# The second norm of the first phase on GpSimd, in groups of 128x384

## The chip, the cores and the metric

One Trainium2 chip, one of its cores. The metric is the device time in microseconds of one execution of the whole kernel. GpSimd is called POOL in the rows, VectorE DVE, ScalarE ACT, TensorE PE (its weight loads PEld), SyncE SP.

## The reference, cut to what matters

The kernel computes two layers on an image batch of 8 x 96 x 128 x 128. The change lies in layer 0, between its convolution and its feed-forward network:

```python
x = x + _L0_conv_ref(_ln_c(x), ...)          # clusters: cosines, sigmoid, argmax mask, gather
t = _to_tokens(x)
t = t + _L0_ffn_ref(_ln_t(t), W1, b1, W2, b2)
x = _from_tokens(t, x)

def _ln_t(v, eps=1e-5):
    m = jnp.mean(v, axis=-1, keepdims=True)
    s = jnp.var(v, axis=-1, keepdims=True)
    return (v - m) / jnp.sqrt(s + eps)
```

The network quantizes its input to fp8 (5 exponent and 2 mantissa bits), multiplies, rounds, applies relu, quantizes again and multiplies again.

## The kernel before, in words

It has three phases, one after the other. The first (`phase_a`) does layer 0 and the first norm of layer 1, the second the depthwise convolutions, the third the rest of layer 1. Only the first is touched.

**Tiles.** The batch is cut into 32 quads (8 images x 4 quarters) of 4096 tokens with 96 channels. A quad in token order is a buffer `xT` of 128 partitions by 32 tokens x 96 channels (3072 fp32). It is handled in 8 groups of 4 tokens per partition (128x384, `CW` = 384, `TPC` = 4, `NK` = 8), and for some work in 2 halves of 16 tokens (128x1536).

**Steps and slots.** A step i works at five quads at once, software-pipelined: the feed-forward network of quad i, the output of the clustering and the statistics of the second norm for quad q1 = i + 1, cosines and similarity for q2 = i + 2, the cluster centres for q3 = i + 3, the load and the statistics of the first norm for q4 = i + 4, and the tail of layer 1's norm for p = i - 1. A step has nine slots, 0 to 8; the network's hidden layer takes group s in slot s, its output group s - 1. Each engine has its order written out by hand: `body` in the block of each engine, with tables such as `COS_AT` (cosines of half 0 in slot 3, of half 1 in slot 5), `SIM_AT` (similarity in slots 4 and 6), `OUT_AT`, `FWD_AT`, `NORM2_AT` (the second norm in slots 7 and 8) and `NORM3_LATE` (ScalarE's third norm of quad p in slots 2 and 3). Nothing plans the order at run time: an engine that waits holds up everything behind it in its list.

**The second norm.** VectorE takes the statistics of a group pair by pair (`pair_stats`, L178) into `ff.st`. GpSimd turns a half of them into `ff.rstd` (`ln2` calls `ln_stats`: a scaling, L163, and a power of -0.5, L166). Then VectorE's `dve_norm` centres a half of the quad into `xc` (L216) and scales it into `q8` as fp8 (L220), half 0 at the end of slot 7 and half 1 at the end of slot 8. TensorE's `pe_q8` (L258) turns the groups of `q8`; that of group 0 of the next quad stands at the end of the step, that of group s + 1 at the start of slot s. It waits for the half that holds the group (event `norm2`, 2 per quad).

**GpSimd's order in a step**, all of it in one list: `ln1(q3, 1)` and `r_by_side(q3, 1)`; `ln3(p, 1)` (L1135 to L1143); `inverse_norms(q2, 0)` and `(q2, 1)` (L1188 to L1205, three Newton steps for rn, which VectorE's `cosines` reads at L987); `ln3(i, 0)`; `scaled_sim(q2, 0)` (L1164); `ln2(q1, 0)`; `centres(q3)`; `scaled_sim(q2, 1)`, which waits for VectorE's similarity in slot 6 (L1014); `ln2(q1, 1)`; `ln1(q4, 0)` and `r_by_side(q4, 0)`. ScalarE's third norm (L856) waits for `ln3`.

Of the kernel before, what the change touches and what calls it, by code (L numbers as in the profile page):

```python
# [5 lines left out]
F32 = mybir.dt.float32  # L6
# [5 lines left out]
ALU = mybir.AluOpType  # L12
# [3 lines left out]
P = 128  # L16
B, C, H, W = 8, 96, 128, 128
# [5 lines left out]
NT = TOK // P  # L23
NK = 8
TPC = NT // NK
CH = TOK // NK
CW = TPC * C
# [74 lines left out]
def begun(unit):  # L102

    return unit.real
# [77 lines left out]
def per_token(t, n):  # L182

    return t.unsqueeze(2).to_broadcast([P, n, C])


class FeedForward:


    def __init__(self, nc, ctx, phase, ev, ring, xT, wts, idb):  # L190
        self.nc, self.ev, self.ring, self.xT, self.w, self.idb = nc, ev, ring, xT, wts, idb
        sb = lambda n, s, d: ctx.enter_context(nc.sbuf_tensor(phase + n, s, d))
        self.hid = ctx.enter_context(nc.psum_tensor(phase + "hid", [P, NJ * CH], F32))
        self.xc = sb("xc", [P, NT // 2, C], F32)
        self.q8 = sb("q8", [P, NT, C], FP8)
        self.q8c = sb("q8c", [C, 2, CH], BF16)
        self.h16 = sb("h16", [P, 2, NJ * CH], F16)
        self.hq = sb("hq", [P, 2, NJ * CH], F16)
        self.y16 = sb("y16", [P, 2, CW], F16)
        self.y16b = sb("y16b", [P, 2, CW], F16)  # L200
        self.st = sb("st2", [P, NT, 3], F32)
        self.rstd = sb("rstd2", [P, NT], F32)
# [2 lines left out]
        return self.xT[i.buf(len(self.xT))]  # L205


    def dve_norm(self, dve, i, half):
        ev, n, o = self.ev, NT // 2, half * (NT // 2)
        x = self.x_of(i)[:, o * C:(o + n) * C].rearrange("p (t c) -> p t c", c=C)  # L210

        dve.wait_ge(ev["ln2"], ev.at("ln2", i, half))
        if half:

            dve.wait_ge(ev["norm2"], ev.at("norm2", i, 0))
        dve.tensor_tensor(self.xc[:], x, per_token(self.st[:, o:o + n, 1], n),  # L216
                          ALU.subtract).then_inc(ev["cen2"], 1)
        dve.wait_ge(ev["cen2"], ev.at("cen2", i, half))
        dve.sem_inc(ev.passed, 1)
        dve.tensor_tensor(self.q8[:, o:o + n, :], self.xc[:], per_token(self.rstd[:, o:o + n], n),  # L220
                          ALU.mult, saturate=False).then_inc(ev["norm2"], 1)

    def dve_hidden(self, dve, i, k):
        ev, b = self.ev, k % 2
# [22 lines left out]
    def pe_q8(self, pe, step, i, k):  # L247
        ev, ring = self.ev, self.ring

        pe.wait_ge(ev["norm2"], ev.at("norm2", i, k // (NK // 2)))  # L250
        name, unit, pos = ring.before(step, "q8", k)
        if begun(unit):

            pe.wait_ge(ev[name], ev.at(name, unit, pos))
        pe.sem_inc(ev.passed, 1)
        bank = ring.bank("q8", k)
        for t in range(TPC):
            m = pe.matmul(bank[0:C, t * P:(t + 1) * P], self.q8[:, k * TPC + t, :], self.idb[:, :],  # L258
                          start=True, stop=True)
        m.then_inc(ev["q8_full"], 1)  # L260
# [60 lines left out]
class SplitFeedForward(FeedForward):  # L321


    def __init__(self, nc, ctx, phase, ev, ring, xT, wts, idb):
        self.nc, self.ev, self.ring, self.xT, self.w, self.idb = nc, ev, ring, xT, wts, idb
        sb = lambda n, s, d: ctx.enter_context(nc.sbuf_tensor(phase + n, s, d))
        self.hid2 = [ctx.enter_context(nc.psum_tensor(phase + f"hid{p}", [P, CH], F32)) for p in range(2)]
        self.xc = sb("xc", [P, NT // 2, C], F32)
        self.q8 = sb("q8", [P, NT, C], FP8)
        self.q8c = sb("q8c", [C, 2, CH], BF16)  # L330
        self.h16 = sb("h16", [P, 2, NJ * CH], F16)
        self.hq = sb("hq", [P, 2, NJ * CH], F16)
        self.y16 = sb("y16", [P, 2, CW], F16)
        self.y16b = sb("y16b", [P, 2, CW], F16)
        self.st = sb("st2", [P, NT, 3], F32)
        self.rstd = sb("rstd2", [P, NT], F32)
# [26 lines left out]
    def dve_hidden(self, dve, i, k):  # L363
        ev, b = self.ev, k % 2
        for j in range(NJ):
# [7 lines left out]
        dve.tensor_scalar(u, u, ROUND8, ROUND8, ALU.add, ALU.subtract).then_inc(ev["hq"], 1)  # L373


FFN_EVENTS = dict(x1=NK, bn2=NK, ln2=2, ln2_s=2, cen2=2, norm2=2, q8_full=NK, y_full=NK, c_full=NK, q8c=NK, hidden=NK, h16=NK,
                  relu=NK, hq=NK, y16=NK, yb=NK, x2=NK, cout=NK)


# [37 lines left out]
COS_AT = {3: 0, 5: 1}  # L417
SIM_AT = {4: 0, 6: 1}
SIMT_AT = {5: 0, 7: 1}
NORM2_AT = {7: 0, 8: 1}  # L420
SIDE_AT, STD_AT, MEAN_AT, CF_AT, CN2_AT, CW_AT = 2, 2, 3, 4, 5, 8
AGG_AT, SUM_AT, VAL_AT, PA_AT = 8, 0, 1, 2
NORM3_AT, NORM3_LATE = {7: (0, 1), 8: (2, 3)}, {2: (4, 5), 3: (6, 7)}
# [2 lines left out]
def phase_a(nc, consts, x, wf_t, wf, bf, wv_t, bv, wp_t, bp, alpha, beta, w1, b1, w2, b2, gamma, beta_ln, x2_dram, x3_dram):  # L426
# [4 lines left out]
    with ExitStack() as ctx:  # L431
        sb = lambda n, s, d: ctx.enter_context(nc.sbuf_tensor(n, s, d))
# [108 lines left out]
        ff = SplitFeedForward(nc, ctx, "A_", ev, back, xT, wts, idb)  # L541
# [387 lines left out]
        def _(dve):  # L929
# [122 lines left out]
            def body(i):  # L1052
                q1, q2, q3, q4, p = i + 1, i + 2, i + 3, i + 4, i - 1
                for s in range(FFN_SLOTS):
# [40 lines left out]
                    if q3.real and s == CW_AT:  # L1095

                        dve.wait_ge(ev["cw"], ev.at("cw", q3, 0))
                        dve.tensor_copy(big_w[:, C:BIGN], s_cw).then_inc(ev["cwc"], 1)  # L1098
                    if q1.real and s in NORM2_AT:
                        ff.dve_norm(dve, q1, NORM2_AT[s])  # L1100

            steps(dve, body)

# [1 line left out]
        def _(pool):  # L1105
# [9 lines left out]
            def ln2(q, half):  # L1115

                pool.wait_ge(ev["bn2"], ev.at("bn2", q, 4 * half + 3))
                pool.sem_inc(ev.passed, 1)
                ln_stats(pool, ev, "ln2", ff.st, ff.rstd, var[1], expo, q, half, EPS_T, 1.0)

# [24 lines left out]
            def r_by_side(q, h):  # L1145

                pool.wait_ge(ev["ln1"], ev.at("ln1", q, h))
                pool.sem_inc(ev.passed, 1)
                if begun(q - 1):

                    pool.wait_ge(ev["side"], ev.at("side", q - 1, 0))
                    pool.sem_inc(ev.passed, 1)
                n = NT // 2
                w = slice(h * n, (h + 1) * n)
                pool.tensor_tensor(rmask[:, w, 2 * h:2 * h + 2], rstd1[q.buf(NB)][:, w].unsqueeze(2).to_broadcast([P, n, 2]),
                                   side.unsqueeze(1).to_broadcast([P, n, 2]), ALU.mult).then_inc(ev["rmask"], 1)
# [50 lines left out]
            def body(i):  # L1207
                q1, q2, q3, q4, p = i + 1, i + 2, i + 3, i + 4, i - 1
                if q3.real:
                    ln1(q3, 1)  # L1210
                    r_by_side(q3, 1)
                if p.real:
                    ln3(p, 1)
                for h in range(2):
                    if q2.real:
                        inverse_norms(q2, h)

                        pool.wait_ge(ev["rn"], ev.at("rn", q2, h))
                        pool.sem_inc(ev.passed, 1)
                if i.real:  # L1220
                    ln3(i, 0)
                if q2.real:
                    scaled_sim(q2, 0)
                if q1.real:
                    ln2(q1, 0)
                if q3.real:
                    centres(q3)
                if q2.real:
                    scaled_sim(q2, 1)
                if q1.real:  # L1230
                    ln2(q1, 1)
                if q4.real:
                    ln1(q4, 0)
                    r_by_side(q4, 0)

            steps(pool, body)


# [636 lines left out]
```

## Time and profile before

| what | us |
|---|---|
| median of 3 runs (range) | 4150.91 (4149.14 to 4152.14) |
| the profiled execution | 4150.77 |
| its span, first to last instruction | 4149.2 |
| first phase, about | 0 to 2105 |

| engine, whole span | busy us | share |
|---|---|---|
| PE | 3270.8 | 79% |
| PEld | 2521.2 | 61% |
| DVE | 3025.8 | 73% |
| ACT | 2745.2 | 66% |
| POOL | 1425.2 | 34% |

The slices of the profile, 40 of 103.7 us each, show the phases; a digit is the busy share in tenths, the first phase is the first twenty:

```
DVE  4888888888888888888852222222288988988987
ACT  2577777777777777777762222222189999999998
POOL 3555655556555565555420000000022222222221
PEclk8788888888888888888769999999889999999999
```

A share is an average over work with different limits. In the first phase no engine is busy all the time, so the order inside one step has to be read.

### The profile page before, as it was taken

Reading aid. Unit: us, or ns where it says so; the run is one execution under the profiler, and the core shown is the slowest. Engines: PE = TensorE matmul, PEld = TensorE weight load, DVE = VectorE, ACT = ScalarE, POOL = GpSimd, SP = SyncE. Lnnn points to the kernel's source line nnn. Section 1 sums busy time; section 2 is a strip of 40 time slices with the busy share of each in tenths; the row PEclk is TensorE's granted clock in tenths of the full one; section 3 lists DMA queues with packets and bytes.
Section 4 is the critical chain, followed back from the end, with each engine's and each line's share of the span. In section 5 each row is a group of like instructions: output and inputs, shape, how many; then the busy total and the mean of one; then the engine's idle time right before and its main releaser. Section 6 shows DMA issues by size and latency. Waiting matters only on the chain. (4 is left out here: it accounts for less than half of the span.)

```text
span 4149.2 us, 80812 instructions
## 1 busy us (share of the span) xinstructions
PE 3270.8 (79%) x26660; PEld 2521.2 (61%) x26660; DVE 3025.8 (73%) x7852; ACT 2745.2 (66%) x6274; POOL 1425.2 (34%) x1892
## 2 busy tenths in 40 slices
PE   6767677776777767777659999999788778787777
PEld 5655555555555555555539999999744444444443
DVE  4888888888888888888852222222288988988987
ACT  2577777777777777777762222222189999999998
POOL 3555655556555565555420000000022222222221
PEclk8788888888888888888769999999889999999999
DMA  3133232332323323232235566566576666666662
GB/s 64 45 77 81 73 77 62 77 80 74 78 62 77 80 75 77 62 78 64 60 102 160 159 165 167 159 165 167 155 199 183 178 177 184 180 180 182 180 180 79
DMA packets 733898, 490.45 MB, mean 118 GB/s; under 512 B 420797, under 2 KB 712957, under 8 KB 721277
## 3 DMA queue, kind: packets, MB, share of 16 engines
q1 hardware_dynamic: 733564, 486.32, 44.5%
q8 instruction: 171, 2.80, 0.3%
q14 instruction: 163, 1.33, 0.1%
HBM read 284.42 MB, written 201.33 MB: 117 GB/s over the span
## 5 line engine op out<-in xcount | busy, mean ns | idle before, releaser
L1794 POOL TENSOR_SCALAR C_var<-C_st 128x16 f32<-128x16 f32 x64 | 16.3, 254 | 1697.4 <-DVE C_st L178 1697.4
L1331 PE MATMUL B_ps_row<-B_g,B_z 128*128 128x128 f32 x4608 | 555.8, 277 | 0.6 <-ACT B_g L1363 0.6
L1331 PEld LDWEIGHTS B_ps_row<-B_g,B_z 128*128 128x128 f32 x4608 | 532.1, 193 | 0.7 <-ACT B_g L1363 0.7
L361 ACT ACTIVATE A_h<-A_hid 128x512 f16<-128x512 f32 x768 | 426.5, 591 | 66.7 <-PE A_hid L348 63.1
L1424 DVE TENSOR_TENSOR B_mid<-B_ps_row,B_row_bias 128x512 f32<-128x512 f32 x192 | 132.8, 691 | 458.3 <-PE B_ps_row L1331 448.3
L166 POOL TENSOR_TENSOR A_rstd<-A_var,A_expo 128x16 f32<-128x16 f32 x128 | 454.2, 3549 | 23.7 <-POOL A_var L163 23.6
L178 DVE BATCH_NORM_STATS2 A_st<-A_xT 128x6 f32<-128x192 f32 x1536 | 443.6, 349 | 24.8 <-ACT A_xT L826 11.5
L361 ACT ACTIVATE C_h<-C_hid 128x512 f16<-128x512 f32 x768 | 426.1, 592 | 15.0 <-PE C_hid L348 7.7
L1461 ACT ACTIVATE C_q<-C_xT,C_shift,C_rstd 128x96 fp8e5<-128x96 f32 x1024 | 391.4, 456 | 40.9 <-POOL C_shift L1801 40.9
L369 DVE TENSOR_SCALAR A_hq<-A_h,A_b 128x512 f16<-128x512 f16 x768 | 250.0, 363 | 198.3 <-ACT A_h L361 193.3
L856 ACT ACTIVATE A_xc<-A_xT,A_shift,A_rstd 128x96 f32<-128x96 f32 x1024 | 379.0, 456 | 0.0
L663 PEld LDWEIGHTS A_fbank<-A_big_w,A_xq 97*128 97x128 f32 x2048 | 337.0, 236 | 63.4 <-DVE A_big_w L1098 29.5
L663 PE MATMUL A_fbank<-A_big_w,A_xq 97*128 97x112 f32 x2048 | 333.9, 318 | 23.2 <-DVE A_big_w L1098 21.7
L1375 ACT ACTIVATE B_y<-B_ps_col,B_col_bias 128x512 f32<-128x512 f32 x192 | 132.0, 687 | 318.1 <-PE B_ps_col L1342 318.1
L348 PE MATMUL A_hid<-A_q8c,A_w 96*128 96x512 bf16 x768 | 313.4, 467 | 31.6 <-ACT A_h L361 29.5
L288 PE MATMUL A_bbank<-A_w,A_hq 128*128 128x96 f16 x3072 | 218.9, 234 | 121.7 <-DVE A_hq L373 73.6
L1645 PE MATMUL C_fbank<-C_y3q,C_pw 96*96 96x512 f32 x512 | 279.5, 629 | 43.1 <-DMA C_y3q<-y_scratch 23.4
L288 PEld LDWEIGHTS A_bbank<-A_w,A_hq 128*128 128x128 f16 x3072 | 189.2, 114 | 188.4 <-DVE A_hq L373 119.3
L348 PE MATMUL C_hid<-C_q8c,C_w 96*128 96x512 bf16 x768 | 262.7, 390 | 49.9 <-ACT C_h L361 43.3
L369 DVE TENSOR_SCALAR C_hq<-C_h,C_b 128x512 f16<-128x512 f16 x768 | 243.1, 346 | 74.1 <-ACT C_h L361 67.8
L296 ACT ACTIVATE A_q8c<-A_bbank 96x512 bf16<-96x512 f32 x256 | 149.8, 586 | 192.6 <-PE A_bbank L258 191.0
L746 PE MATMUL A_fbank<-A_pabd,A_simT 128*128 128x384 f32 x512 | 234.6, 587 | 35.5 <-DVE A_xT L1050 35.5
(162 smaller groups left out, 7509.5 us busy)
## 6 DMA issues: line engine op xcount, KB each, us to landing
A_xq<-in_x SPq DMA_DIRECT2D x32, 1536.0 KB, 8.9
x_scratch<-A_xT SPq DMA_DIRECT2D x64, 768.0 KB, 3.2
x_scratch<-A_x3h SPq DMA_DIRECT2D x64, 768.0 KB, 5.4
B_z<-x_scratch SPq DMA_DIRECT2D x96, 512.0 KB, 5.0
y_scratch<-B_y SPq DMA_DIRECT2D x96, 512.0 KB, 3.7
C_x3q<-x_scratch SPq DMA_DIRECT2D x32, 1536.0 KB, 9.2
C_y3q<-y_scratch SPq DMA_DIRECT2D x32, 1536.0 KB, 15.7
C_xT<-x_scratch SPq DMA_DIRECT2D x64, 768.0 KB, 15.9
```

Source lines behind the costliest of these rows:

```text
L166: m = pool.tensor_tensor(rstd[:, o:o + n], var[:], expo[:, 0:n], ALU.pow)
L178: return dve.bn_stats(st[:, n:n + 2, :].rearrange("p t s -> p (t s)"), x[:, n * C:(n + 2) * C].rearrange("p (t c) -> p c t", t=2))
L288: m = pe.matmul(bank[:, t * C:(t + 1) * C], self.hq[:, b, s:s + P], self.w["w2"][:, j, :], start=(j == 0), stop=(j == NJ - 1))
L348: pe.matmul(self.hid2[n % 2][:], self.w["w1"][:, j * P:(j + 1) * P], self.q8c[:, k % 2, :], start=True, stop=True).then_inc(ev["hidden"], 1)
L361: act.activation(self.h16[:, k % 2, j * CH:(j + 1) * CH], self.hid2[n % 2][:], ACT.Copy).then_inc(ev["h16"], 1)
L369: r = dve.tensor_scalar(self.hq[:, b, s], self.h16[:, b, s], self.w["b1"][:, j:j + 1], 0.0, ALU.add, ALU.max)
L663: m = pe.matmul(bank[:, t * BIGN:(t + 1) * BIGN], xq[q.buf(NX)][:, n * P:(n + 1) * P], big_w[:, :], start=True, stop=True)
L746: pe.matmul(front.bank("out", k)[:, 0:CW], simT[q.buf(2)][:, k, :], pabd[:], start=True, stop=True).then_inc(ev["out_full"], 1)
L856: m = act.activation(xc3[:, k // 4, t % (NT // 2), :], xT[u.buf(NB)][:, t * C:(t + 1) * C], ACT.Identity, scale=rstd3[:, t:t + 1], bias=sh ...
L1331: m = pe.matmul(ps_row[h][:, b * P:(b + 1) * P], z[c.buf(NB)][:, h * HB + b, d:d + W], g[c.buf(2)][:, d, :], start=(d == 0), stop=(d == 2))
L1461: m = act.activation(self.q8[:, t, :], x[:, t * C:(t + 1) * C], ACT.Identity, scale=self.rstd[:, t:t + 1], bias=self.shift[:, t:t + 1], sa ...
L1645: pe.matmul(rows(front.bank("pw", k)[0:C, 0:CH]), pw[:], group(y3q[q.buf(2)], k), start=True, stop=True).then_inc(ev["pw_full"], 1)
```

## The change

`dve_norm` and its table `NORM2_AT` are gone. `pool_norm` does the same arithmetic on GpSimd, a half per call and within it a group at a time: centring (subtract the mean) of group k + 1 is put ahead of scaling (multiply by rstd, to fp8) of group k, with two group buffers in `xc`. The call for half 0 of quad q1 stands in GpSimd's list behind `ln2(q1, 1)`, the call for half 1 of quad i near the start of the list, behind `r_by_side(q3, 1)` and ahead of `ln3(p, 1)`. The events `cen2` and `norm2` count 8 per quad in place of 2, and TensorE waits for the group it reads. `ln2` waits until the norm of the quad before has read `rstd`.

```diff
-        self.xc = sb("xc", [P, NT // 2, C], F32)
+        self.xc = sb("xc", [P, 2, TPC, C], F32)
...
-    def dve_norm(self, dve, i, half):
-        ev, n, o = self.ev, NT // 2, half * (NT // 2)
-        x = self.x_of(i)[:, o * C:(o + n) * C].rearrange("p (t c) -> p t c", c=C)
-
-        dve.wait_ge(ev["ln2"], ev.at("ln2", i, half))
-        if half:
-
-            dve.wait_ge(ev["norm2"], ev.at("norm2", i, 0))
-        dve.tensor_tensor(self.xc[:], x, per_token(self.st[:, o:o + n, 1], n),
-                          ALU.subtract).then_inc(ev["cen2"], 1)
-        dve.wait_ge(ev["cen2"], ev.at("cen2", i, half))
-        dve.sem_inc(ev.passed, 1)
-        dve.tensor_tensor(self.q8[:, o:o + n, :], self.xc[:], per_token(self.rstd[:, o:o + n], n),
-                          ALU.mult, saturate=False).then_inc(ev["norm2"], 1)
+    def pool_norm(self, pool, i, half):
+        ev, x = self.ev, self.x_of(i)
+        first = half * NK // 2
+
+        def centred(k):
+            if k >= 2:
+
+                pool.wait_ge(ev["norm2"], ev.at("norm2", i, k - 2))
+            elif begun(i - 1):
+                pool.wait_ge(ev["norm2"], ev.at("norm2", i - 1, NK - 2 + k))
+            t = slice(k * TPC, (k + 1) * TPC)
+            pool.tensor_tensor(self.xc[:, k % 2], x[:, k * CW:(k + 1) * CW].rearrange("p (t c) -> p t c", c=C),
+                               per_token(self.st[:, t, 1], TPC), ALU.subtract).then_inc(ev["cen2"], 1)
+
+        def scaled(k):
+
+            pool.wait_ge(ev["cen2"], ev.at("cen2", i, k))
+            if begun(i - 1):
+
+                pool.wait_ge(ev["q8_full"], ev.at("q8_full", i - 1, k))
+            t = slice(k * TPC, (k + 1) * TPC)
+            pool.tensor_tensor(self.q8[:, t, :], self.xc[:, k % 2], per_token(self.rstd[:, t], TPC), ALU.mult,
+                               saturate=False).then_inc(ev["norm2"], 1)
+
+        pool.wait_ge(ev["ln2"], ev.at("ln2", i, half))
+        centred(first)
+        for k in range(first, first + NK // 2):
+            if k + 1 < first + NK // 2:
+                centred(k + 1)
+            scaled(k)
...
-        pe.wait_ge(ev["norm2"], ev.at("norm2", i, k // (NK // 2)))
+        pe.wait_ge(ev["norm2"], ev.at("norm2", i, k))
...
-                    if q1.real and s in NORM2_AT:
-                        ff.dve_norm(dve, q1, NORM2_AT[s])
...
                 pool.wait_ge(ev["bn2"], ev.at("bn2", q, 4 * half + 3))
+                if begun(q - 1):
+
+                    pool.wait_ge(ev["norm2"], ev.at("norm2", q - 1, 4 * half + 3))
...
                     ln1(q3, 1)
                     r_by_side(q3, 1)
+                if i.real:
+                    ff.pool_norm(pool, i, 1)
                 if p.real:
                     ln3(p, 1)
...
                     ln2(q1, 1)
+                    ff.pool_norm(pool, q1, 0)
                 if q4.real:
                     ln1(q4, 0)
```

## Rows read from the trace of the kernel before

**Rows 1.** One line's instructions, 300 to 2000 us: count, min/median/max ns, first and last start.

```profile
L1014 DVE TENSOR_TENSOR A_sim<-A_sim,A_eq x53: 424/425/426, 302.7 to 1987.8; 128x256 f32<-128x256 f32 x53
```

**Rows 2.** Stretches of one step: length, busy us (instructions) by engine, granted clock, DMA share, GB/s.

```profile
1016.53:1031.93 15.40, 11.99 (x141) 10.11 (x141) 14.94 (x32) 11.68 (x27) 11.98 (x9) 0.82 0.24 75
1031.93:1049.69 17.76, 14.43 (x155) 12.85 (x155) 12.57 (x36) 11.49 (x31) 11.46 (x20) 0.71 0.12 26
1049.69:1081.38 31.69, 20.93 (x155) 14.19 (x155) 28.21 (x86) 23.70 (x55) 13.78 (x23) 0.87 0.44 101
```

**Rows 3.** VectorE in order of time: start, us, instruction, count, [idle before <-releaser].

```profile
1016.11 0.42 DVE L1014 TENSOR_TENSOR A_sim<-A_sim,A_eq 128x256 f32<-128x256 f32 x1
...
1021.38 1.75 DVE L216 TENSOR_TENSOR A_xc<-A_xT,A_st 128x1536 f32<-128x1536 f32 x1
1023.28 1.76 DVE L220 TENSOR_TENSOR A_q<-A_xc,A_rstd 128x1536 fp8e5<-128x1536 f32 x1 [0.15 <-DVE A_xc L216]
...
1028.36 1.75 DVE L216 TENSOR_TENSOR A_xc<-A_xT,A_st 128x1536 f32<-128x1536 f32 x1
1030.26 1.76 DVE L220 TENSOR_TENSOR A_q<-A_xc,A_rstd 128x1536 fp8e5<-128x1536 f32 x1
...
1049.69 0.23 DVE L987 TENSOR_TENSOR A_rn<-A_rn,A_guard 128x64 f32<-128x64 f32 x1
...
1059.82 0.35 DVE L369 TENSOR_SCALAR A_hq<-A_h,A_b 128x512 f16<-128x512 f16 x1 [2.16 <-ACT A_h L361]
```

**Rows 4.** GpSimd in order of time, same step; then the spread of L163.

```profile
1016.71 0.62 POOL L1164 TENSOR_TENSOR A_simr<-A_sim,A_rstd 128x256 f32<-128x256 f32 x1 [6.30 <-DVE A_sim L1014]
...
1017.73 2.90 POOL L166 TENSOR_TENSOR A_rstd<-A_var,A_expo 128x16 f32<-128x16 f32 x1 [0.18 <-POOL A_var L163]
1021.23 0.21 POOL L163 TENSOR_SCALAR A_var<-A_st 128x16 f32<-128x16 f32 x1 [0.60 <-DVE A_st L178]
1021.63 4.26 POOL L166 TENSOR_TENSOR A_rstd<-A_var,A_expo 128x16 f32<-128x16 f32 x1 [0.18 <-POOL A_var L163]
...
1028.43 1.75 POOL L163 TENSOR_SCALAR A_var<-A_st 128x16 f32<-128x16 f32 x1 [1.63 <-DVE A_st L178]
1030.37 4.41 POOL L166 TENSOR_TENSOR A_rstd<-A_var,A_expo 128x16 f32<-128x16 f32 x1 [0.18 <-POOL A_var L163]
...
1039.54 0.64 POOL L1143 TENSOR_TENSOR A_shift<-A_less,A_rstd 128x16 f32<-128x16 f32 x1 [0.18 <-POOL A_rstd L1140]
1041.97 0.26 POOL L1188 TENSOR_SCALAR A_guard<-A_rstd 128x16 f32<-128x16 f32 x1 [1.79 <-DVE A_seed L978]
...
1047.88 0.32 POOL L1205 TENSOR_TENSOR A_rn<-A_newton 128x64 f32<-128x64 f32 x1 [0.18 <-POOL A_newton L1202]
...
L163 POOL TENSOR_SCALAR A_var<-A_st x109: 207/263/1779, 303.9 to 2094.5; 128x16 f32<-128x16 f32 x109
```

**Rows 5.** ScalarE in order of time, same step: third norm in slot 2, slot 3's first copy.

```profile
1045.44 2.96 ACT L856 ACTIVATE A_xc<-A_xT,A_shift,A_rstd 128x96 f32<-128x96 f32 x8
...
1048.60 0.57 ACT L296 ACTIVATE A_q8c<-A_bbank 96x512 bf16<-96x512 f32 x1
```

**Rows 6.** GpSimd's nearest passes: one line's instructions, columns as in rows 1.

```profile
L1164 POOL TENSOR_TENSOR A_simr<-A_sim,A_rstd x55: 618/622/787, 303.3 to 2046.7; 128x256 f32<-128x256 f32 x55
...
L1205 POOL TENSOR_TENSOR A_rn<-A_newton x52: 317/320/323, 334.5 to 1967.5; 128x64 f32<-128x64 f32 x52
```

**Rows 7.** VectorE's spread, 300 to 2100 us: one line's instructions, columns as in rows 1.

```profile
L991 DVE TENSOR_TENSOR A_dots<-A_dots,A_rn x54: 424/576/890, 336.6 to 2033.3; 128x256 f32<-128x256 f32 x54
...
L369 DVE TENSOR_SCALAR A_hq<-A_h,A_b x675: 330/346/772, 303.0 to 2094.6; 128x512 f16<-128x512 f16 x169
...
L373 DVE TENSOR_SCALAR A_hq<-A_hq x225: 559/560/857, 304.4 to 2095.0; 128x1536 uint16<-128x1536 uint16 x113
...
L240 DVE TENSOR_TENSOR A_y16b<-A_y,A_b x225: 343/351/455, 304.9 to 2095.5; 128x384 f16<-128x384 f16 x113
...
L244 DVE TENSOR_TENSOR A_xT<-A_xT,A_y16b x225: 557/558/667, 305.3 to 2095.9; 128x384 f32<-128x384 f32 x113
```

More of the change, by code:

```diff
@@ L327, in __init__ @@
         self.hid2 = [ctx.enter_context(nc.psum_tensor(phase + f"hid{p}", [P, CH], F32)) for p in range(2)]
-        self.xc = sb("xc", [P, NT // 2, C], F32)
+        self.xc = sb("xc", [P, 2, TPC, C], F32)
         self.q8 = sb("q8", [P, NT, C], FP8)
@@ L373, in dve_hidden @@
         dve.tensor_scalar(u, u, ROUND8, ROUND8, ALU.add, ALU.subtract).then_inc(ev["hq"], 1)
-FFN_EVENTS = dict(x1=NK, bn2=NK, ln2=2, ln2_s=2, cen2=2, norm2=2, q8_full=NK, y_full=NK, c_full=NK, q8c=NK, hidden=NK, h16=NK,
+FFN_EVENTS = dict(x1=NK, bn2=NK, ln2=2, ln2_s=2, cen2=NK, norm2=NK, q8_full=NK, y_full=NK, c_full=NK, q8c=NK, hidden=NK, h16=NK,
                   relu=NK, hq=NK, y16=NK, yb=NK, x2=NK, cout=NK)
@@ L419 @@
 SIMT_AT = {5: 0, 7: 1}
-NORM2_AT = {7: 0, 8: 1}
 SIDE_AT, STD_AT, MEAN_AT, CF_AT, CN2_AT, CW_AT = 2, 2, 3, 4, 5, 8
```

## The prediction

> **What bounds the kernel now.** I read the slices and the stretches first, then one steady step on each engine in order of time, then the spread of single instructions. The first phase ends at about 2105 us and is a loop over 32 quads; the change touches nothing behind it. Its period is 64.8 us: the last pass of the similarity of a quad half (L1014) comes 53 times between 302.7 and 1987.8 us, two to a step, so 1685.1 / 26 [rows 1]. I call S the end of its second half in slot 6 (1016.53 in the step read) and divide the step there. From S to the first cosines of the next step (L987, slot 3, 1049.69) are 33.2 us, from there to the next S 31.7 us [rows 2, 3]. In the second part VectorE is busy for 28.2 of 31.7 us and its only long wait, 2.16 us, is for ScalarE: VectorE bounds it. In the first part it is busy almost throughout up to the end of slot 8 (14.9 of 15.4 us), then 12.6 of 17.8 us while it follows ScalarE and TensorE [rows 2, 3].
>
> GpSimd is busy for 12.0 + 11.5 + 13.8 = 37.3 of 64.8 us [rows 2]. Its share says there is room for the new passes. What decides is where they stand in its order, since it is served in order by a written list, and two others wait for its results: VectorE's cosines of slot 3 need the inverse norms (L1205 to A_rn), and ScalarE's third norm in slot 2 needs the rstd and shift of ln3 (L1143). Today these come in time: the inverse norms end at 1048.20 with the cosines at 1049.69, and ln3's shift ends at 1040.18 with its reader at 1045.44 [rows 3, 4, 5].
>
> **What is removed.** Four passes of 128x1536 on VectorE per step: 2 x 1.75 + 2 x 1.76 = 7.0 us, all of them between S and slot 3 [rows 3]. They lie on the path today: behind them VectorE copies the summed rows and starts the next slot. So VectorE would be at slot 3 up to 7.0 us earlier; with the order of ScalarE and TensorE as it stands I expect half of that to come back as waits for ScalarE: it arrives between S + 26.2 (33.2 - 7.0, no new wait) and S + 33.2 (all of it given back), say S + 29.5.
>
> **What is added.** Sixteen passes of 128x384 on GpSimd per step, eight at the end of the list (half 0 of the next quad, behind ln2) and eight near its start (half 1, behind ln1 and ahead of ln3 and of both inverse norms). No such pass is in the trace. The nearest rows are the pass of 128x256 with a broadcast operand, 0.618 at the least, 0.622 in the median, and the one of 128x64, 0.320 [rows 6]. Their slope is 0.302 / 192 = 1.57 ns an element, which gives 0.62 + 128 x 0.00157 = 0.82 us for 384. The lower bound is 0.62 (it can't be shorter than the smaller pass); the upper is 0.622 x 384 / 256 = 0.93 with nothing fixed in it. The scaling pass writes fp8 instead of fp32, and no row shows that on GpSimd; VectorE's own passes differ by 0.02 us for it [rows 3], so I add nothing and keep 1.0 us as an outer end. The GPSIMD Engine Reference of the Trainium skill (section Performance versus the Vector engine) gives 4497 ns for 2048 elements, an estimate of 0.84 us for 384 by proportion; by it the sum below would be 0.3 us longer a step. Waiting for the instruction just ahead costs GpSimd 0.18 us each time; a half has two or three such places. So a half costs 8 x 0.82 + 3 x 0.18 = 7.1 us, or 6.9, together 14.0 us.
>
> **The chain on GpSimd from S to the cosines.** Today: scaled similarity, ln2, ln1 of half 0, ln1 of half 1, ln3, inverse norms, from 1016.53 to 1048.20, 31.7 us [rows 3, 4]. Three idle times in it vanish when the engine runs late: 0.60 before L163, 1.63 between 1026.80 and 1028.43, and 1.79 before L1188, 4.0 us. Three of its instructions are long today because VectorE's big passes run: L163 takes 1.75 in place of 0.25 and ends with the L216 beside it (1030.18 against 1030.11), and L166 takes 4.26 and 4.41 where it takes 2.90 alone, both beside an L216 or L220 [rows 3, 4]. With those passes gone this gives back 1.50 + 1.36 + 1.51 = 4.4 us. So 31.7 - 4.0 - 4.4 + 14.0 = 37.3 us, and with 0.1 to VectorE 37.4 us. VectorE can be there at S + 29.5. It therefore stands at slot 3 for about 8 us in every step, and ScalarE stands in slot 2: ln3 ends ahead of the inverse norms by their 6.2 us (1041.97 to 1048.20), at S + 31.2, where ScalarE gets to its reader at S + 28.9 today (1045.44) and would some 3 us earlier now. From ln3's end ScalarE needs 2.96 and 0.2 us to slot 3's first copy [rows 5], so at S + 34.4 it is 3.0 us ahead of the cosines, against 1.1 us today: this lead takes most of the 2.16 us wait in slot 4 [rows 3, 5]. The second part becomes 30.0 us (between 29.5 and 31.7).
>
> **Waits for the port.** The row of L163 shows what a GpSimd read meets when VectorE runs with two SBUF inputs: it ends when VectorE's does. The other way round, L991 takes 0.424 at the least but 0.576 in the median and 0.890 at most, and L369 up to 0.772 for 0.346 [rows 4, 7]. So the two engines wait for each other's whole instructions, and the new passes will meet those of VectorE. Of that kind VectorE has in each slot 3 x 0.35 + 0.56 + 0.35 + 0.56 = 2.5 us (L369, L373, L240, L244) [rows 7]. SBUF — State Buffer of the Trainium skill (section Who interferes with whom) says the same as a rule: a VectorE instruction with two SBUF inputs or in a two-port mode and a GpSimd one that reads SBUF exclude each other for a whole instruction. While half 0 is normed (S + 4 to S + 12) VectorE has an addition pair (L240, L244) and part of a hidden block in its way, 1.5 us; while half 1 is normed (about S + 22 to S + 30) more than one slot's worth, 2.7 us. I take 4.2 us a step for both, between 0 (every pass in a gap) and 8 us (each of the 16 passes held for most of an instruction of 0.56). What VectorE itself loses, half a pass of 0.82 each time, falls ahead of its stall in slot 3 and costs nothing.
>
> **The sum.** Period 37.4 + 4.2 + 30.0 = 71.6 us, 6.8 more than today. The chain has both ln1 calls and both norms in the steps i = 0 to 28, 29 of them: +197 us. The last three steps lack ln1 and the inverse norms, so VectorE's relief counts there, between 0 and 21 us; I take 10. The profiled execution is 4150.8 us with a span of 4149.2, and the median of the runs is 4150.9, so no correction between them: 4150.8 + 197 - 10 = 4338, about 4340 us.
>
> The other edits cost nothing I can find. TensorE's wait by group (k in place of the half) waits for group 0, done after ln2 (S + 4.1) and three passes, S + 7; today the half is done at 1025.04, S + 8.5 [rows 3]. Groups 4 to 7 are done when ln3 begins, S + 27 to S + 31, and are first asked for in slot 3. The new wait of ln2 on the norms of the last quad is over long before. Nothing of the DMA queues moves: the stores of x2 and x3 only follow the later steps.
>
> **The rivals.**
> 1. The chain binds, but the port waits are near nothing and the pass takes 0.82: period 37.4 + 30.0 = 67.4, so 29 x 2.6 - 10 = +65, 4216 us. For it: the last instruction of the inverse norms hardly varies beside a busy VectorE (317 to 323 ns) [rows 6]. Against: L163's row.
> 2. The passes are slow: 1.0 us each (+2.9 a step), 6 us of port waits and no gain of lead: 37.4 + 2.9 + 6 + 31.7 = 78.0, 29 x 13.2 - 10 = +373, 4524 us. It needs fp8 output to be dear on GpSimd or VectorE to win the port always.
> 3. The other side: the norm is hidden on GpSimd and VectorE's relief counts. It decides at the chain's length: with 30.0 us behind it, the period falls below 64.8 once the sixteen passes and their port waits take less than 11.4 us (0.66 us a pass, no port wait); at the bound of 0.62 it gives 64.2, 29 x -0.6 - 10 = -27, about 4123 us. Were it fully hidden, VectorE at S + 29.5 would give 61.1, 3.7 less in 29 steps, 4040 us. The slope of rows 6 speaks against both.
> 4. Nearly no change, 4150 within 8 us: the narrow strip between rivals 1 and 3.
>
> **Chances.** Forecast (4260 to 4450) 0.62; rival 1 (4160 to 4260) 0.15; rival 2 (above 4450) 0.12; rival 3 0.07; rival 4 0.04. The range 4190 to 4460 leaves out about 2 in 10. A measurement of this kernel can tell about 0.2% (8 us) from no change: faster 0.07, same 0.04, slower 0.89.
>
> **What the profile after would show.** L216 and L220 gone from VectorE; sixteen passes of 0.8 to 1.0 us on GpSimd per step, with a longer tail where VectorE works; L166 back at 2.9 us; VectorE before L987 idle for 7 to 12 us a step with GpSimd's A_rn as releaser (today: none); ScalarE before L856 waiting for A_shift L1143; GpSimd's idle before L1188 nearly gone; TensorE's granted clock lower in slot 3. I am wrong if L987 has no wait, if the pass takes under 0.66 us, or if the stall comes elsewhere, at q8 of a group.

## The result, and the profile after

The changed kernel takes 4266.59 us (median of 4 runs, 4264.12 to 4268.1) against 4150.89 before: 1.0278 times as long, 95% interval 1.0261 to 1.0296. It is slower by 116 us. The prediction said slower, 4340 us, range 4190 to 4460; the direction and the place were right, the size was too large by 73 us.

The whole loss lies in the first phase: the last similarity of a quad (L1014, now L1029) starts at 2160.9 us in place of 2046.1, and VectorE's first instruction of the second phase comes at 2281.3 in place of 2161.0.

The same two stretches of a step as in [rows 2], of the kernel after (S to the cosines, cosines to the next S; columns as there):

```profile
1004.23:1041.58 37.35, 27.64 (x303) 24.61 (x304) 24.37 (x62) 24.74 (x62) 32.57 (x44) 0.77 0.16 44
1041.58:1072.85 31.27, 21.74 (x150) 14.83 (x149) 28.15 (x87) 21.20 (x48) 13.71 (x23) 0.83 0.44 101
```

The first stretch was 33.2 us and is 37.35, the second was 31.7 and is 31.3. Over the 24 to 26 steady steps between 300 and 2100 us, with S (the end of the similarity) and the start of the first cosines taken for each step, the means are 33.2 + 31.7 before (period 64.8) and 37.6 + 30.9 after (period 68.55). All means by step below are worked out in this way. The stretch from S to the cosines is called the first part below, the rest of the step the second part.

Waits of the kernel after, 300 to 2100 us (engine, line waited for: us in total, times, longest):

```profile
DVE A_rn L1002 <- POOL A_rn L1221: 140.1, 26, 6.2
...
ACT A_xc L871 <- POOL A_shift L1159: 146.6, 26, 6.3
```

VectorE waits for the inverse norms in slot 3, 140.1 / 26 = 5.4 us a step, where the line before (L987) had no wait in these steps. ScalarE waits for ln3 in slot 2, 5.6 us a step. Each is one wait per step.

GpSimd's list in the same step, in order of time (start, us, instruction, count), and the spread of the two new passes, 300 to 2100 us (min/median/max ns):

```profile
1004.40 0.62 POOL L1180 TENSOR_TENSOR A_simr<-A_sim,A_rstd 128x256 f32<-128x256 f32 x1 [6.30 <-DVE A_sim L1029]
...
1008.29 1.83 POOL L219 TENSOR_TENSOR A_xc<-A_xT,A_st 128x384 f32<-128x384 f32 x2
...
1015.86 2.90 POOL L166 TENSOR_TENSOR A_rstd<-A_var,A_expo 128x16 f32<-128x16 f32 x1 [0.18 <-POOL A_var L163]
...
1041.23 0.32 POOL L1221 TENSOR_TENSOR A_rn<-A_newton 128x64 f32<-128x64 f32 x1 [0.18 <-POOL A_newton L1218]
...
L219 POOL TENSOR_TENSOR A_xc<-A_xT,A_st x208: 825/832/1227, 322.9 to 2057.0; 128x384 f32<-128x384 f32 x104
L229 POOL TENSOR_TENSOR A_q<-A_xc,A_rstd x208: 818/827/1142, 324.7 to 2059.0; 128x384 fp8e5<-128x384 f32 x104
```

A pass takes 0.83 us in the median, with fp8 output too. One pass in three takes longer, up to 1.23 us; the mean is 0.91 us. From S (1004.23) the chain runs to the end of the inverse norms at 1041.55 with no pause longer than 0.28 us. The power of ln1 is back at 2.90 us where [rows 4] had 4.26 and 4.41.

VectorE in the same step:

```profile
1024.33 1.07 DVE L389 TENSOR_SCALAR A_hq<-A_hq 128x1536 uint16<-128x1536 uint16 x1
...
1028.14 1.07 DVE L260 TENSOR_TENSOR A_xT<-A_xT,A_y16b 128x384 f32<-128x384 f32 x1
...
1029.85 2.10 DVE L385 TENSOR_SCALAR A_hq<-A_h,A_b 128x512 f16<-128x512 f16 x3
...
1041.58 0.23 DVE L1002 TENSOR_TENSOR A_rn<-A_rn,A_guard 128x64 f32<-128x64 f32 x1 [5.20 <-POOL A_rn L1221]
```

Beside the passes of half 1 (1024.0 to 1031.5) VectorE's instructions take twice their time and more: 1.07 for 0.56, 2.10 for 0.87. In the whole first part it is busy for 24.4 us, where the kernel before has 27.5 with 7.0 of them in the norm [rows 2, 3]: 3.9 us more for the same instructions. It pays for the port, and then stands 5.20 us in slot 3 anyhow.

### The profile page after: what moved, and what is told of

It is laid out like the page before. It is cut to its first block and busy times, and to the rows that moved or that the text cites. A ratio compares the mean times of both kernels' runs of the same rounds, so it can differ in the third digit from the quotient of the medians.

```text
span 4266.2 us, 81411 instructions
## 1 busy us (share of the span) xinstructions
PE 3273.9 (77%) x26660; PEld 2544.5 (60%) x26660; DVE 2921.9 (68%) x7724; ACT 2744.7 (64%) x6274; POOL 1728.3 (41%) x2404
## 5 line engine op out<-in xcount | busy, mean ns | idle before, releaser
L385 DVE TENSOR_SCALAR A_hq<-A_h,A_b 128x512 f16<-128x512 f16 x768 | 288.9, 413 | 281.6 <-ACT A_h L377 274.7
L364 PE MATMUL A_hid<-A_q8c,A_w 96*128 96x512 bf16 x768 | 291.2, 434 | 196.5 <-ACT A_h L377 194.6
L166 POOL TENSOR_TENSOR A_rstd<-A_var,A_expo 128x16 f32<-128x16 f32 x128 | 377.9, 2953 | 24.0 <-POOL A_var L163 24.0
L678 PEld LDWEIGHTS A_fbank<-A_big_w,A_xq 97*128 97x128 f32 x2048 | 354.1, 248 | 33.1 <-issue 8.4
L678 PE MATMUL A_fbank<-A_big_w,A_xq 97*128 97x112 f32 x2048 | 351.1, 331 | 4.9 <-DVE A_pabd L1058 3.5
L304 PEld LDWEIGHTS A_bbank<-A_w,A_hq 128*128 128x128 f16 x3072 | 198.5, 117 | 198.0 <-DVE A_hq L389 112.9
L761 PE MATMUL A_fbank<-A_pabd,A_simT 128*128 128x384 f32 x512 | 247.5, 615 | 29.9 <-DVE A_xT L1065 29.9
L1382 ACT ACTIVATE B_g<-B_ps_g 128x384 f32<-128x384 f32 x96 | 47.2, 491 | 303.4 <-PE B_ps_c L1337 303.4
```

The lines of the kernel that those rows point to most:

```text
L166: m = pool.tensor_tensor(rstd[:, o:o + n], var[:], expo[:, 0:n], ALU.pow)
L304: m = pe.matmul(bank[:, t * C:(t + 1) * C], self.hq[:, b, s:s + P], self.w["w2"][:, j, :], start=(j == 0), stop=(j == NJ - 1))
L364: pe.matmul(self.hid2[n % 2][:], self.w["w1"][:, j * P:(j + 1) * P], self.q8c[:, k % 2, :], start=True, stop=True).then_inc(ev["hidden"], 1)
L385: r = dve.tensor_scalar(self.hq[:, b, s], self.h16[:, b, s], self.w["b1"][:, j:j + 1], 0.0, ALU.add, ALU.max)
L678: m = pe.matmul(bank[:, t * BIGN:(t + 1) * BIGN], xq[q.buf(NX)][:, n * P:(n + 1) * P], big_w[:, :], start=True, stop=True)
L761: pe.matmul(front.bank("out", k)[:, 0:CW], simT[q.buf(2)][:, k, :], pabd[:], start=True, stop=True).then_inc(ev["out_full"], 1)
```

## The experiments

Two theories were to be told apart. **Order:** the loss is the place of the sixteen passes in GpSimd's list, inside the chain from S to the inverse norms; VectorE's relief is real but spent as waiting. **Amount of work and port:** GpSimd has got too much to do, or holds the port too long, wherever the passes stand. Each time stands beside 7 to 17 runs of the kernel before on the same chip (medians 4150.0 to 4151.6).

### VectorE's relief alone

```diff
+        x, n = x[:, 0:1, :], 1
-        dve.tensor_tensor(self.xc[:], x, per_token(self.st[:, o:o + n, 1], n),
+        dve.tensor_tensor(self.xc[:, 0:1, :], x, per_token(self.st[:, o:o + n, 1], n),
...
-        dve.tensor_tensor(self.q8[:, o:o + n, :], self.xc[:], per_token(self.rstd[:, o:o + n], n),
+        dve.tensor_tensor(self.q8[:, o:o + n, :], self.xc[:, 0:1, :], per_token(self.rstd[:, o:o + n], n),
```

> The kernel before, with VectorE's four passes of the second norm cut from 128x1536 to 128x96 (the rest of the norm is left out, the waits stay). No pass goes to GpSimd. It prices VectorE's relief alone. Order theory (what the changed kernel lost, it lost by the place of its passes in GpSimd's list; the relief itself is real): VectorE spends about 1 instead of 7 us on the norm, reaches slot 3 at S + 30 in place of S + 33.2, the second part stays at 31.3 us, so the period is 61 to 62 us against 64.8 and the whole 4050 to 4080 us. Rival (ScalarE and TensorE set the first part anyway, so that VectorE's relief is worth next to nothing and the changed kernel could only lose): 4130 to 4150 us.

Measured 4054.34 us, ratio 0.9769 (0.9753 to 0.9786), in the expected range. Stretches of one step:

```profile
1032.91:1063.28 30.37, 25.44 (x297) 22.29 (x297) 21.79 (x68) 22.81 (x58) 18.80 (x28) 0.80 0.19 54
1063.28:1094.22 30.94, 20.63 (x155) 14.15 (x154) 28.27 (x87) 22.85 (x53) 13.62 (x23) 0.89 0.45 103
```

The mean period is 61.4 us. Six microseconds less on VectorE shorten the first part by 2.8 us (33.2 to 30.4): less than half counts, the rest comes back as waits for ScalarE and TensorE. The relief is worth 97 us, so the changed kernel had something to win.

### The same passes elsewhere in GpSimd's list

Half 0 behind ln2 of half 0, where GpSimd waits:

```diff
                     ln2(q1, 0)
+                    ff.pool_norm(pool, q1, 0)
...
                     ln2(q1, 1)
-                    ff.pool_norm(pool, q1, 0)
```

> The changed kernel with the norm of half 0 of the next quad moved in GpSimd's list from behind ln2 of half 1 to behind ln2 of half 0, where the engine waits for VectorE for 2.3 and 6.3 us. The same sixteen passes, the same waits. Order theory: the chain from S to the inverse norms is shorter by 7.1 us, 30.2 us, so VectorE arrives last, at S + 31; the passes now meet VectorE where it is the bound and cost it 1 to 3 us there; period 63.5 to 65.5, the whole 4110 to 4175 us. Rival (the loss comes from the amount of work on GpSimd and the port it holds, wherever it stands): 4250 to 4280 us, as changed.

Groups 5 to 7 of half 1 behind the inverse norms (`pool_norm` takes its first group and a count):

```diff
                 if i.real:
-                    ff.pool_norm(pool, i, 1)
+                    ff.pool_norm(pool, i, 1, 4, 1)
...
                         pool.wait_ge(ev["rn"], ev.at("rn", q2, h))
                         pool.sem_inc(ev.passed, 1)
+                    if i.real:
+                        ff.pool_norm(pool, i, 1, 5 + h, 1 + h)
```

> The changed kernel with three of the four groups of half 1 taken out of the chain in GpSimd's list: group 4 stays, group 5 goes behind the first inverse norms, groups 6 and 7 behind the second. Order theory: the chain from S is shorter by three groups, 5.3 us, 32.0 us, as long as VectorE needs to get there (S + 32.2); the wait at the cosines, 5.4 us a step, goes; period 63.5 to 65, the whole 4115 to 4160 us. Rival (amount of work and port): 4250 to 4280 us.

Both moves:

> Both moves together: half 0 behind ln2 of half 0, groups 5 to 7 behind the inverse norms. Order theory: the chain from S is 24.9 us and no longer binds anywhere; VectorE does, with 6 us less work and what it loses by the port: period 61.5 to 64.5, the whole 4060 to 4140 us, below e2 and e3 only if VectorE's arrival is not what ends the first part in those. Rival (amount of work and port): 4250 to 4280 us.

Measured 4181.60 us with half 0 early (e2; ratio 1.0076, 1.0060 to 1.0093), 4154.22 us with groups 5 to 7 late (e3; 1.0007, 0.9997 to 1.0016) and 4206.74 us with both (e4; 1.0132, 1.0115 to 1.0149). One step of each, in this order:

```profile
1026.68:1058.74 32.06, 26.68 (x296) 23.59 (x296) 22.57 (x64) 22.87 (x58) 25.68 (x36) 0.76 0.18 51
1058.74:1093.35 34.61, 21.73 (x155) 15.10 (x155) 31.08 (x87) 23.76 (x56) 20.64 (x31) 0.80 0.40 92
```

```profile
1020.13:1052.52 32.39, 27.42 (x318) 24.28 (x319) 22.66 (x62) 24.72 (x64) 27.40 (x38) 0.81 0.18 51
1052.52:1084.99 32.47, 17.88 (x134) 11.96 (x132) 30.30 (x87) 21.98 (x49) 19.63 (x29) 0.87 0.43 99
```

```profile
1040.25:1071.55 31.30, 26.34 (x296) 23.33 (x296) 21.45 (x63) 22.84 (x58) 21.97 (x32) 0.77 0.19 52
1071.55:1107.93 36.38, 24.37 (x155) 16.79 (x155) 33.13 (x87) 24.09 (x56) 25.05 (x36) 0.73 0.39 88
```

With the same sixteen passes the loss falls from 116 us to 30, to 3 and to 55. The first part shrinks each time, in the mean from 37.6 to 31.3, 32.2 and 30.6 us, as the order theory says; the amount-of-work theory, which expected 4250 to 4280 in all three, falls. But the second part grows, from 30.9 to 34.0, 32.6 and 35.8 us, and VectorE's busy time in it, in the steps shown, from 28 to 31, 30 and 33 us for the same 87 instructions. There VectorE is the bound, and the passes are beside it. The port half of the rival is therefore right in that part: e2 and e4 lie above what I expected (4110 to 4175, 4060 to 4140), since I had priced the meeting at 1 to 3 us.

Two waits are left in e3 that its expectation did not have. VectorE still stands for the inverse norms, 52.1 / 26 = 2.0 us a step. And TensorE waits for the late groups of `q8` in the second part, 134.8 us in the 26 steps, 5.2 a step (e4: 61.7 us, 2.4). VectorE is busy there for 30.3 of 32.5 us, so this second wait can account for 2.2 us at most; no run takes it away by itself.

### The port by itself

The kernel before with eight passes that nobody uses, behind ln2 of half 0:

```diff
+            def extra(q):
+                for k in range(8):
+                    if k >= 2:
+                        pool.wait_ge(ev["dum"], ev.at("dum", q, k - 2))
+                    elif begun(q - 1):
+                        pool.wait_ge(ev["dum"], ev.at("dum", q - 1, 6 + k))
+                    pool.tensor_tensor(scr[:, k % 2], scr_in[:], per_token(expo[:, 0:TPC], TPC),
+                                       ALU.mult).then_inc(ev["dum"], 1)
...
                     ln2(q1, 0)
+                    extra(q1)
```

> The kernel before, whole, with eight more passes of 128x384 on GpSimd that nobody uses, with two SBUF operands, behind ln2 of half 0, where GpSimd waits for VectorE for more than their 7.1 us. They prolong no chain. Port theory (what e2, e3 and e4 lost behind the cosines is VectorE waiting for the port): VectorE's instructions there take 2.5 to 3.5 us a step longer, period 67.3 to 68.3, the whole 4225 to 4265 us. Rival (e2 and e4 lost it because results of GpSimd, the centres and the scaled similarity, came later or because of TensorE's lower clock): 4150 to 4180 us.

And the same with fills in place of the passes:

```diff
+                    pool.memset(scr[:, k % 2], 0.0).then_inc(ev["dum"], 1)
```

> As the run with eight unused passes, but the passes only write (a fill of 128x384), so they read nothing from SBUF. Port theory with a lock of the reading side for instructions with two SBUF operands and of both sides for the fast one-operand forms: the additions (L240, L244) keep their 0.35 and 0.56 us, the fast forms (L369, L373) still wait; the loss is half of that with reading passes or less, 4160 to 4210 us. If any GpSimd instruction shuts VectorE out: as with reading passes, in proportion to the fills' length. If no write does: 4145 to 4160 us.

Measured 4256.18 us with passes (1.0261, 1.0243 to 1.0278) and 4153.56 us with fills (1.0006, 0.9997 to 1.0016). With the passes, the second stretch of a step, VectorE in slot 6, and the pass's spread:

```profile
1032.83:1067.90 35.07, 22.11 (x155) 15.20 (x155) 31.53 (x87) 23.77 (x56) 20.55 (x31) 0.79 0.39 91
```

```profile
1056.09 2.53 DVE L369 TENSOR_SCALAR A_hq<-A_h,A_b 128x512 f16<-128x512 f16 x3
1058.65 1.06 DVE L373 TENSOR_SCALAR A_hq<-A_hq 128x1536 uint16<-128x1536 uint16 x1
1059.64 0.98 DVE L240 TENSOR_TENSOR A_y16b<-A_y,A_b 128x384 f16<-128x384 f16 x1
1060.65 1.06 DVE L244 TENSOR_TENSOR A_xT<-A_xT,A_y16b 128x384 f32<-128x384 f32 x1
...
L1216 POOL TENSOR_TENSOR A_scr<-A_scr_in,A_expo x200: 821/870/1138, 303.2 to 1947.8; 128x384 f32<-128x384 f32 x100
```

Four lines of VectorE take 2.53 + 1.06 + 0.98 + 1.06 = 5.6 us, where slot 5 of the same step has 0.87 + 0.56 + 0.35 + 0.56 = 2.3. These 3.3 us are nearly all of the 3.4 us by which the mean second part is longer (35.0 against 31.7); the mean period is 68.2 against 64.8. GpSimd's passes themselves stay at 0.87 us in the median, 0.90 in the mean, for 0.82 at the least. No data depended on these passes. The cluster centres behind them in the list end some 5 us later in the step (30.5 us behind the first cosines in place of 25.7), but between 300 and 2000 us no other engine waits for any result of GpSimd. So this is the price of the port alone: 106 us.

With fills, these are their spread and VectorE's, 300 to 2000 us:

```profile
L1216 POOL MEMSET A_scr<- x208: 412/413/608, 357.1 to 1981.2; 128x384 f32 x104
...
L369 DVE TENSOR_SCALAR A_hq<-A_h,A_b x627: 332/347/1385, 303.0 to 1989.0; 128x512 f16<-128x512 f16 x157
...
L240 DVE TENSOR_TENSOR A_y16b<-A_y,A_b x210: 337/351/500, 304.8 to 1995.0; 128x384 f16<-128x384 f16 x105
...
L244 DVE TENSOR_TENSOR A_xT<-A_xT,A_y16b x210: 557/558/666, 305.2 to 1995.3; 128x384 f32<-128x384 f32 x105
```

The additions with two SBUF inputs (L240, L244) reach 0.50 and 0.67 us at most, much as in [rows 7] (0.46 and 0.67), where the reading passes held them up to 0.98 and 1.07. The fast one-input form (L369) is held, up to 1.39 us for 0.35. So a write shuts out the fast form and a read both. SBUF — State Buffer of the Trainium skill (section Who interferes with whom) states this split; the trace agrees. The fills cost nothing in all, 3 us within the interval, less than I had expected of the fast forms (4160 to 4210 us). By the time alone the case in which no write shuts VectorE out (4145 to 4160) would have won; the row of L369 speaks against it. The second part does get longer, 32.3 us in the mean for 31.7, and the first gives the same back, 32.5 for 33.2; why it does was not tried.

### A microsecond in the chain

The changed kernel with the same fills, which cost nothing elsewhere, put ahead of ln3:

```diff
                 if i.real:
                     ff.pool_norm(pool, i, 1)
+                if i.real:
+                    extra(i)
                 if p.real:
                     ln3(p, 1)
```

> The changed kernel with the eight unused fills of 128x384 (0.413 us each, the ones that cost nothing behind ln2 of half 0) put ahead of ln3, inside the chain. They shut nobody out of SBUF. Order theory: every microsecond there is a microsecond of the period: 8 x 0.413 = 3.3 us a step, the whole 4345 to 4385 us. Port or amount-of-work rival: 4260 to 4275 us.

Measured 4365.43 us (1.0516, 1.0500 to 1.0533), 99 us more than the changed kernel. VectorE's wait for the inverse norms, 300 to 2000 us:

```profile
DVE A_rn L1005 <- POOL A_rn L1224: 164.3, 23, 9.0
```

7.1 us a step in place of 5.4, and a mean period of 71.7 against 68.55, 3.1 us for 3.3 us of fills. Free in one place of the list, paid nearly in full in another: this shows the chain as the cause, without the reading side of the port. The expectation says that the fills shut nobody out of SBUF; the row of L369 above shows that VectorE's fast form does wait for them, which cost nothing there in all.

### The wait by group

```diff
-        pe.wait_ge(ev["norm2"], ev.at("norm2", i, k))
+        pe.wait_ge(ev["norm2"], ev.at("norm2", i, 4 * (k // 4) + 3))
```

> The changed kernel with TensorE waiting again for the half that holds the group (the fourth norm of the half in place of its own). Order theory: q8 of group 0 then goes at S + 11.3 in place of S + 8.7, which shifts slots 0 to 2 by up to 2.6 us, but GpSimd's chain ends 5.4 us behind VectorE: same time, 4255 to 4280 us. Rival (the group wait is what kept the loss small): 2 us or more a step, above 4320 us.

Measured 4245.34 us (1.0229, 1.0213 to 1.0245): 21 us less than the changed kernel, which neither theory said. TensorE does wait for the half, 300 to 2000 us:

```profile
PE A_bbank L274 <- POOL A_q L229: 68.9, 25, 3.2
```

2.8 us a step, and yet the mean period is 67.4 us (66.0 to 68.7 from step to step) with 37.3 + 30.1. So the finer wait did not keep the loss small. Most of the gain stands in the second part, where VectorE waits 0.7 us a step for ScalarE's copies (A_h) in place of 1.6; and GpSimd's passes take 0.88 us in the mean in place of 0.91. Why the coarse wait does this is open; the later start changes where TensorE idles and with that its granted clock, but nothing here isolates that.

### One half only

Half 1 on VectorE in slot 8, half 0 on GpSimd as changed (the other half's call dropped, each engine with events of its own):

```diff
                     if q1.real and s == 8:
+                        ff.dve_norm(dve, q1, 1)
...
-                if i.real:
-                    ff.pool_norm(pool, i, 1)
```

> Half of the change: half 0 is normed on GpSimd as in the changed kernel (behind ln2 of half 1), half 1 stays with VectorE in slot 8, in passes of 128x1536. Order theory: GpSimd's chain from S is 23.4 + 7.1 = 30.5 us, but VectorE's two passes of slot 8 meet GpSimd's and hold them up to 3.5 us, 31 to 34; VectorE itself arrives at S + 31.5 to 32.5; behind it 31.0. Period 63 to 65, the whole 4090 to 4155 us. Amount-of-work rival: half way between before and changed, 4205 us.

Half 0 on VectorE in slot 7, half 1 on GpSimd as changed:

```diff
                     if q1.real and s == 7:
+                        ff.dve_norm(dve, q1, 0)
...
                     ln2(q1, 1)
-                    ff.pool_norm(pool, q1, 0)
```

> The other half of the change: half 1 is normed on GpSimd as in the changed kernel (ahead of ln3), half 0 stays with VectorE in slot 7, in passes of 128x1536. Order theory: the chain from S is 23.4 + 6.9 + 1.5 for the passes of slot 7 = 31.8 us, VectorE arrives at S + 31.5 to 32.5, behind it 31.0: period 62.7 to 63.8, the whole 4080 to 4120 us, a little below the kernel before and below e5. Amount-of-work rival: 4205 us.

Measured 4136.98 us for the first (e5; 0.9969, 0.9959 to 0.9980) and 4129.63 us for the second (e6; 0.9952, 0.9936 to 0.9969), 10 us above what I had expected of it. Both beat the kernel before by a little, 0.3 and 0.5%; half the work moved is not half the loss, the amount-of-work theory's 4205 is out. One step of the second:

```profile
1009.29:1042.61 33.32, 27.39 (x313) 23.91 (x314) 24.87 (x65) 24.72 (x62) 26.62 (x36) 0.81 0.18 49
1042.61:1072.59 29.98, 19.58 (x141) 12.89 (x139) 28.32 (x87) 21.70 (x51) 14.27 (x23) 0.90 0.47 107
```

In the mean 33.8 + 30.2: the chain still ends last (VectorE waits 84.5 / 26 = 3.3 us a step for it), 2.0 us later than I had summed, since GpSimd's idle times of 0.60 and 1.63 us had come back, and the gain lies in the second part. There VectorE's wait for ScalarE's copies (A_h) falls from 2.35 us a step before the change to 0.8.

### Half 1 before the second ln1

```diff
                     r_by_side(q3, 1)
-                if i.real:
-                    ff.pool_norm(pool, i, 1)
...
                     ln1(q4, 0)
                     r_by_side(q4, 0)
+                if q1.real:
+                    ff.pool_norm(pool, q1, 1)
```

> The kernel with half 0 on VectorE and half 1 on GpSimd (e6), with the norm of half 1 moved from behind the second ln1 to ahead of it, at the end of the step before, into the 1.63 us in which GpSimd waits for VectorE's statistics. Order theory: the chain from S shrinks from 33.7 to 32 us, VectorE arrives at 31.5 to 32: period 62.0 to 62.8 against 64.0, the whole 4070 to 4100 us. If VectorE already ended the first part in e6: 4120 to 4135 us. It is the version that may beat both kernels.

Measured 4150.16 us (1.0000, 0.9991 to 1.0009): a miss. GpSimd's chain did shrink to 32.3 us and VectorE no longer waits for it, but VectorE comes only at S + 32.8 itself (33.0 in the mean), and the second part is 31.8 us in place of 30.2: VectorE waits 2.5 us a step there for ScalarE's copies in place of 0.8. VectorE in slot 0, then the wait of TensorE that hangs on it, here and in the kernel of half 1 (e6), 300 to 2000 us:

```profile
1025.70 1.66 DVE L402 TENSOR_SCALAR A_hq<-A_h,A_b 128x512 f16<-128x512 f16 x2
...
1028.14 0.96 DVE L402 TENSOR_SCALAR A_hq<-A_h,A_b 128x512 f16<-128x512 f16 x1 [0.78 <-ACT A_h L394]
1029.14 1.06 DVE L406 TENSOR_SCALAR A_hq<-A_hq 128x1536 uint16<-128x1536 uint16 x1
...
PE A_fbank L735 <- DVE A_summed L1060: 75.2, 26, 2.9
```

```profile
PE A_fbank L735 <- DVE A_summed L1060: 52.3, 27, 2.3
```

The passes now stand beside slot 0, where TensorE waits for VectorE's copy of the summed rows: three lines take 3.7 us where e6 has 1.5, and TensorE waits 2.9 us in place of 1.9. Its granted clock in the first part is 0.76 in the mean, as before the change, in place of 0.82: in pieces of 2 us from S, it is at the lower level (0.50 to 0.53, 1.2 GHz) from S + 16 to S + 26 here and to S + 22 in e6, behind an idle time that ends at S + 17.6 here and at S + 16.3 there. Between S + 14 and S + 30 it is at the lower level for 10.2 us in every step here, as before the change, and for 4.6 us in the mean in e6 (0.9 to 6.8).

### One group late

The kernel of half 1 with its last group behind the first inverse norms:

```diff
-                    ff.pool_norm(pool, i, 1)
+                    ff.pool_norm(pool, i, 1, 4, 3)
...
                         pool.wait_ge(ev["rn"], ev.at("rn", q2, h))
                         pool.sem_inc(ev.passed, 1)
+                    if i.real and h == 0:
+                        ff.pool_norm(pool, i, 1, 7, 1)
```

> The kernel with half 0 on VectorE and half 1 on GpSimd (e6), with the last of its four groups moved behind the first inverse norms. Order theory: the chain from S is shorter by one group, 1.8 us (33.7 to 31.9), VectorE arrives at S + 31.5 to 32.5, and one group's two passes meet VectorE behind the cosines, 0.55 us: period 63.0 to 63.8 against 64.0, the whole 4100 to 4125 us. If the run with half 1 first showed that there is nothing to win before S + 32.8, the two prices nearly cancel: 4125 to 4140 us.

Measured 4091.51 us, ratio 0.9855 (0.9839 to 0.9871), the best of all complete kernels, 59 us below the one before. A step:

```profile
990.84:1022.90 32.06, 24.71 (x307) 21.49 (x308) 25.59 (x65) 24.10 (x61) 25.15 (x34) 0.87 0.18 51
1022.90:1053.46 30.56, 21.15 (x147) 14.15 (x145) 29.47 (x87) 22.03 (x50) 15.73 (x25) 0.83 0.46 104
```

The mean is 32.1 + 30.6 = 62.7 us: the first part gives 1.7 us, the second takes 0.4 back for the one group. The whole is 9 us below the range that I gave, and the mean period 0.3 us below it.

## Why the prediction was right, and where its size was off

The direction, the place and the forecast case (4260 to 4450) came true. The size did so with luck: the predicted period was 3.05 us too large, 88 us over the 29 steps, and the ends of the phase were 22 us too small, which took a quarter of that back.

- **The bound and the place.** Right. The cosines wait for the inverse norms (5.4 us a step, expected 7 to 12) and ScalarE for ln3 (5.6 us), none of it before. Shown by the fills in the chain (99 us) against the same fills behind ln2 (3 us), and by the moved passes. The wait at the cosines is shorter than forecast, since the chain is, and since VectorE comes later.
- **What VectorE gains.** Right: I had it at S + 29.5; with the relief alone it arrives at S + 30.4, with 1 of 7 us still spent. In the changed kernel it is done with slot 2 at S + 32.2 (1036.38), since it pays for the port on the way.
- **The pass.** 0.82 us by the slope of [rows 6], 0.83 measured in the median; fp8 output costs nothing (0.827 against 0.832). The estimate by the figure in the GPSIMD Engine Reference of the Trainium skill (section Performance versus the Vector engine), 0.84, would have done as well.
- **The chain.** I had 37.4 us without port waits and 41.6 with them; it is 37.35 in the step read and 37.6 in the mean, port waits and all. The idle times and the prolonged powers went as summed. Two smaller things made room: the passes follow each other without the 0.18 us waits that the sum had put in (0.9 us a step), and two short instructions are shorter than in the step read of the kernel before (the shift of ln3 0.22 us for 0.64, the first Newton product 0.29 for 0.59).
- **The port waits: the term that was mis-sized.** I put 4.2 us a step on GpSimd's chain. The sixteen passes take 0.911 us in the mean where the shortest takes 0.82: 1.4 us a step. With the 0.9 us of waits that weren't there, the two halves, 7.1 (1008.29 to 1015.39) and 7.5 us (1024.02 to 1031.51), come out 0.6 us above the 14.0 of the sum. That the engines shut each other out was right, and that what VectorE loses costs nothing here, since it stands in slot 3 afterwards; how the loss is shared was wrong. VectorE bears most of it, 3.9 us in the first part of the step read. The row of L163 in [rows 4] had shown VectorE's 1.75 us passes ahead of a single small GpSimd instruction; back-to-back GpSimd passes of 0.83 us beside short VectorE instructions are another case. The run with unused passes shows the same: passes at 0.90 us in the mean, 0.6 us a step in all, VectorE 3.3 us a step longer.
- **The second part.** I took 30.0 us; it is 30.9. ScalarE's lead was to take most of VectorE's wait in slot 4; that wait fell only from 2.35 to 1.6 us a step. So the first part is 4.0 us too large, the second 0.9 too small, and the period of 71.6 us exceeds the measured 68.55 by 3.05.
- **The ends.** I took 10 us off for the last steps. By the measured period, 29 steps give 29 x 3.74 = 108 us, while the second phase starts 120.3 us later (2281.3 against 2161.0); the later phases are 3 us shorter. So the ends of the first phase cost some 12 us more in place of 10 less; 5.5 of them lie behind the last similarity (the delay up to it is 114.8 us). Why VectorE's relief is not seen there was not tried.
- **The rivals.** 4267 lies at the lower end of the case forecast (4260 to 4450), and its mechanism is nearer to the first rival, port waits near nothing on GpSimd, than to the forecast. In the terms of the forecast, what happened is rival 1's mechanism with a period of 68.55 us for its 67.4. Rival 3, a faster kernel, would have needed a period shorter by another 3.75 us. With all sixteen passes on GpSimd no order that was run got below the kernel before (4154.22 us is the best); with eight of them three did.
- **The other edits.** Costed at nothing; the wait by group turned out to cost 21 us against the wait by half. The step that failed is that I looked only for lateness; what the runs show in its place is VectorE's longer wait for ScalarE in the second part (1.6 against 0.7 us a step). Why the finer wait brings it stays open.

## What to carry to other kernels

Ask of work moved to an idle engine where it stands in that engine's order, not how full the engine is: write down the chain from the last thing it waits for to the first result that others wait for, and take off what the change removes from it. Then ask whom the moved work meets: beside an engine that is the bound, a shared port can be paid by that engine, though the moved instructions look nearly untouched (here 3.3 us a step on VectorE, 0.6 on GpSimd). Part of a move can win where the whole loses; here a half with one group set apart gave 1.45%.

## What the runs showed of the hardware that I had not expected

- In a meeting of back-to-back GpSimd passes (128x384, 0.83 us) with VectorE's instructions, GpSimd keeps nearly its pace (0.87 us in the median of the unused passes) and VectorE waits for most of a pass: L240 up to 0.98 us for 0.35, L244 up to 1.07 for 0.56. I had expected GpSimd to lose much more.
- A GpSimd fill of 128x384 takes 0.413 us, half of a pass with two inputs, and leaves VectorE's two-input additions alone; only the fast one-input form waits.
- TensorE's granted clock enters as a second-order term: of two kernels that differ in the place of one call, the one whose TensorE waited 1 us longer ran its next stretch at 1.2 GHz for some 4 us longer in the step read, and for 10.2 us in place of 4.6 in the mean. That this is what took the gain of the run with half 1 first is argued from the two traces, not shown by a run of its own.
